# Sigmoid on ScalarE, a last norm in one step, and a ternary layer quantised two tiles ahead

## The reference, cut to what matters

```python
# second layer, attention: a from 12 heads over the tokens, a1 over 100 memory slots
alpha = sigmoid(concat([a, a1]) @ w_alpha + b_alpha)
fused = alpha * a + (1.0 - alpha) * a1
h = h + (fused @ w_proj + b_proj)
# ternary feed-forward, on x = _layernorm(h)
def act_quant(x):
    scale = 127.0 / clip(max(abs(x), axis=-1), 1e-05, None)
    return clip(round(x * scale), -128.0, 127.0) / scale
def bitlinear(x, w, g):              # w is rounded to -1, 0, 1 times one scale
    xn = x * rsqrt(mean(x * x) + 1e-6) * g
    return act_quant(xn) @ weight_quant(w).T
hid = gelu(bitlinear(x, w1, g1))     # 192 -> 768
h = h + bitlinear(hid, w2, g2)       # 768 -> 192
```

## Time and profile before

| what | us |
|---|---|
| median of 3 runs | 1982.28 (1982.16 to 1995.48) |
| the profiled execution | 1991.73 |
| its span, first to last instruction | 1989.9 |
| mean granted clock of TensorE | 0.878 |
| stretch behind attention, pair 1 | 847 to 1028 |
| stretch behind attention, pair 2 | 1810 to 1987 |

### The profile page before, as it was taken

The page is one execution under the profiler, slowest core; times in us unless marked ns, Lnnn a source line. Parts: engine busy times, 40 slices in busy tenths (PEclk is TensorE's granted clock), DMA queues, the critical chain, the costliest instruction groups (busy, mean ns, idle before and its releaser), DMA issues.

```text
span 1989.9 us, 26444 instructions
## 1 busy us (share of the span) xinstructions
PE 1642.2 (83%) x9798; PEld 919.7 (46%) x9798; DVE 1356.8 (68%) x3076; ACT 971.2 (49%) x1383; POOL 126.8 (6%) x165
## 2 busy tenths in 40 slices
PE   0769878998999999964457898799999999999454
PEld 0348646654333333363243584656534333336323
DVE  4668663046889989677768477422588998984876
ACT  0422452124777777732532324330567777775153
POOL 5010000000000000005020100000000000000200
PEclk9977796998999999986568787899989999999656
DMA  6003210016010010001010312000510100100001
GB/s 149 1 1 112 68 44 0 1 35 187 25 32 25 25 32 25 1 1 32 0 33 0 99 45 67 13 0 1 179 60 25 32 25 27 30 9 1 0 0 32
DMA packets 53894, 73.39 MB, mean 37 GB/s; under 512 B 18712, under 2 KB 27205, under 8 KB 53767
## 3 DMA queue, kind: packets, MB, share of 16 engines
q1 hardware_dynamic: 52150, 68.54, 11.9%
q0 software_dynamic: 1616, 3.16, 0.7%
HBM read 38.51 MB, written 33.17 MB: 36 GB/s over the span
## 4 chain that ended last, share of the span: by engine, by line
PE 64%; DVE 26%; ACT 4%; issue 3%; DMA 2%; SPq 1%; POOL 0%; DVEq 0%; ACTq 0%
PE PV L905 9%; PE ST L889 8%; PE S L855 6%; PE ST L801 4%; PE ST L556 4%; PE MT L855 3%; PE PV L914 2%; DVE nmp L1529 2%; DVE Er L1605 2%; DVE st L1402 2%; PE S L812 2%; DVE R L1625 2%; DVE amax L1626 2%; PE ST L586 1%; PE S L850 1%
## 5 line engine op out<-in xcount | busy, mean ns | idle before, releaser
L1232 ACT ACTIVATE Er<-ST 128x1024 f32<-128x1024 f32 x384 | 377.1, 1021 | 106.2 <-PE ST L889 105.9
L1581 DVE TENSOR_REDUCE nmp<-S 128x1 f32<-128x512 f32 x514 | 337.7, 683 | 30.5 <-PE S L855 30.5
L889 PE MATMUL ST<-QS,KS 100*128 100x512 bf16 x768 | 218.0, 385 | 0.3
L905 PE MATMUL PV<-Er,V 128*17 128x512 f32 x1536 | 212.1, 602 | 0.0
L855 PE MATMUL S<-KS,QS 96*128 96x512 bf16 x514 | 183.3, 392 | 0.8
L1581 DVE TENSOR_REDUCE nmp<-MT 128x1 f32<-128x512 f32 x254 | 173.6, 683 | 13.5 <-PE MT L855 13.5
L855 PEld LDWEIGHTS S<-KS,QS 96*128 96x128 bf16 x514 | 48.2, 98 | 154.9 <-DVE nmp L1581 107.2
L450 POOL TENSOR_SCALAR tp<-mv 128x8 f32<-128x8 f32 x20 | 5.2, 258 | 1693.1 <-DVE mv L1406 1693.1
L1529 DVE TENSOR_REDUCE nmp<-S 128x1 f32<-128x512 f32 x120 | 77.5, 684 | 48.3 <-PE S L671 48.1
L889 PEld LDWEIGHTS ST<-QS,KS 100*128 100x128 bf16 x768 | 72.1, 99 | 64.2 <-ACT Er L1232 5.7
L855 PE MATMUL MT<-KS,QS 96*128 96x512 bf16 x254 | 99.4, 391 | 0.9 <-DVE nmp L1581 0.9
(11 more groups left out here) (386 smaller groups left out, 3210.9 us busy)
## 6 DMA issues: line engine op xcount, KB each, us to landing
KS<-scr_k SPq DMA_DIRECT2D x72, 192.0 KB, 2.7
scr_k<-R SPq DMA_DIRECT2D x16, 576.0 KB, 4.0
QS<-scr_q SPq DMA_DIRECT2D x48, 192.0 KB, 2.8
scr_k<-R SPq DMA_DIRECT2D x16, 384.0 KB, 4.6
QS<-scr_k SPq DMA_DIRECT2D x24, 192.0 KB, 2.4
scr_q<-R SPq DMA_DIRECT2D x8, 576.0 KB, 4.5
scr_k<-R SPq DMA_DIRECT2D x16, 192.0 KB, 5.2
scr_q<-R SPq DMA_DIRECT2D x8, 384.0 KB, 4.7
```

What stands on the lines that cost most here:

```text
L889: ins = nc.tensor.matmul(ST[i % 2][:, (kt % 2) * HALF:(kt % 2 + 1) * HALF], KS[0:KP + 4, k, kt * P:(kt + 1) * P], QS[0:KP + 4, k, half * H ...
L905: ins = nc.tensor.matmul(PV[row:row + VC, :], slots[h // H].V[:, kt, h % H, :], E[:, step % RING, (kt % 2) * HALF:(kt % 2 + 1) * HALF], st ...
L1232: A_(E[:, g, :], ST[i % 2][:, :], ACT.Exp).then_inc(s["exps"], 1)
L1581: v.tensor_reduce(nmp[:, u // 2, u % 2:u % 2 + 1], bank, AX.X, ALU.max).then_inc(s["reduced"], 1)
```

## The change

- ScalarE takes Sigmoid instead of exp(-x); VectorE's add of 1 and its reciprocal go. The difference of `U` and `X` is a function of its own (`differ`), made for both slots as soon as a slot's turns (jobs 4 and 5) are done.
- The last norm: `centre` subtracts the mean and multiplies by the weight in one step for each tile (scalar_tensor_tensor) and takes the largest magnitude; it waits for the statistics alone. `quantise` multiplies the magnitude and the scale by `rnn` in small steps, and scales a tile with `MAGIC` added, unlinked; it signals after each half (`scaled`). ScalarE takes `MAGIC` away (`unscale`: Identity with a bias column) for half a slot at a time.
- The order: VectorE adds slot z's projection before slot a's norm. ScalarE makes unscale(a), qcopy(a), unscale(z), Gelu of a's first tile, qcopy(z), Gelu of z's first tile. TensorE makes a's first `bit_up` before z's turns. In the ternary layer VectorE quantises tiles 0 and 1 ahead of the spread of tile 4, and so on.

```diff
--- before.py
+++ after.py
@@ -160,6 +160,7 @@
...
         wsum = sb("wsum", [P, 2])
+        unmagic = sb("unmagic", [P, 1])
@@ -251,7 +252,7 @@
...
             units0 reduced0 units reduced rowmax mturned mcopied acc0 ctxr accout st0 ex0 pv0 ctxn ctxt ctxtc att atts
-            pooled mixin mixed merged stile exps pv alpha alphae fusedx fproj h3 quant qturned qcopied
+            pooled mixin mixed merged stile exps pv alpha alphae fusedx fproj h3 scaled quant qturned qcopied
             vlink plink filled pp pa pd kr0 kr1 kr2 kr3 qr0 qr1 qr2 qr3 q0w q0r mw mr""".split()
@@ -986,7 +987,7 @@
...
                     half, c = i // 2, i % 2
-                    pe.wait_ge(s["quant"], at(p, o, 8, 4 * half + 4))
+                    pe.wait_ge(s["quant"], at(p, o, 2, half + 1))
                     if i >= 2:
@@ -1084,7 +1085,8 @@
...
                     turn_quant(p, o)
-                for t in range(HT):
+                    bit_up(p, o, 0)
+                for t in range(1, HT):
                     for o in slots:
@@ -1249,6 +1251,18 @@
...
+            def unscale(p, o):
+                for half in range(2):
+                    act.wait_ge(s["scaled"], at(p, o, 2, half + 1))
+                    A_(o.XQ[:, HT * half:HT * half + HT, :], o.X[:, HT * half:HT * half + HT, :], ACT.Identity, scale=1.0, bias=unmagic[:, 0:1]).then_inc(s["quant"], 1)
+            def qcopy(p, o):
+                for i in range(4):
+                    half, c = i // 2, i % 2
+                    act.wait_ge(s["qturned"], at(p, o, 4, i + 1))
+                    A_(o.XQT[:, c, half * HALF:(half + 1) * HALF], o.D2[i % 2][0:CH, :].bitcast(BF16)[:, 0:HALF], ACT.Copy).then_inc(s["qcopied"], 1)
             def bit_gelu(p, o, t):
@@ -1318,15 +1332,16 @@
...
                             act.wait_ge(s["fusedx"], at(p, o, 4, i - 1))
-                        A_(o.e2[:, i % 2, :, :], o.D2[i % 2][:, 0:2 * D].rearrange("p (t d) -> p t d", t=2), ACT.Exp, scale=-1.0).then_inc(s["alphae"], 1)
+                        A_(o.e2[:, i % 2, :, :], o.D2[i % 2][:, 0:2 * D].rearrange("p (t d) -> p t d", t=2), ACT.Sigmoid).then_inc(s["alphae"], 1)
                 for o in slots:
                     evac(p, o, 6, o.XT)
-                for o in slots:
-                    for i in range(4):
-                        half, c = i // 2, i % 2
-                        act.wait_ge(s["qturned"], at(p, o, 4, i + 1))
-                        A_(o.XQT[:, c, half * HALF:(half + 1) * HALF], o.D2[i % 2][0:CH, :].bitcast(BF16)[:, 0:HALF], ACT.Copy).then_inc(s["qcopied"], 1)
-                for t in range(HT):
+                unscale(p, a)
+                qcopy(p, a)
+                unscale(p, z)
+                bit_gelu(p, a, 0)
+                qcopy(p, z)
+                bit_gelu(p, z, 0)
+                for t in range(1, HT):
                     for o in slots:
@@ -1351,6 +1366,7 @@
...
+            v.memset(unmagic[:], -MAGIC)
             v.memset(nmp[:], 0.0).then_inc(s["reduced"], 2)
@@ -1595,30 +1611,41 @@
...
+            def differ(p, o):
+                ve.wait_ge(o.s["turned"], p * 28 + 24)
+                for i in range(4):
+                    own, mem = o.U[:, 2 * i:2 * i + 2, :], o.X[:, 2 * i:2 * i + 2, :]
+                    ins = v.tensor_tensor(own, own, mem, ALU.subtract)
+                link(ins)
             def fuse(p, o):
...
                     own, mem = o.U[:, 2 * i:2 * i + 2, :], o.X[:, 2 * i:2 * i + 2, :]
-                    v.tensor_scalar(e, e, 1.0, None, ALU.add)
-                    link(v.tensor_tensor(own, own, mem, ALU.subtract))
-                    link(v.reciprocal(e, e))
                     link(v.tensor_tensor(own, own, e, ALU.mult))
...
+            def centre(p, o):
+                ve.wait_ge(o.s["stats"], p * 5 + 5)
+                for t in range(T):
+                    ins = v.scalar_tensor_tensor(out=o.X[:, t, :], in0=o.HS[:, t, :], scalar=o.mv[:, t, 0:1], in1=g1bc[:], op0=ALU.subtract, op1=ALU.mult)
+                link(ins)
+                link(v.tensor_reduce(o.amax[:], o.X[:], AX.X, ALU.max, apply_absolute_value=True))
             def quantise(p, o):
                 ve.wait_ge(o.s["rstd"], p * 5 + 5)
-                for t in range(T):
-                    ins = v.tensor_scalar(o.X[:, t, :], o.HS[:, t, :], o.mv[:, t, 0:1], o.rnn[:, t:t + 1], ALU.subtract, ALU.mult)
-                link(ins)
-                link(v.tensor_tensor(o.X[:], o.X[:], g1bc[:].unsqueeze(1).to_broadcast([P, T, D]), ALU.mult))
-                link(v.tensor_reduce(o.amax[:], o.X[:], AX.X, ALU.max, apply_absolute_value=True))
+                link(v.tensor_tensor(o.amax[:], o.amax[:], o.rnn[:], ALU.mult))
                 link(v.tensor_scalar(o.qinv[:], o.amax[:], 1e-5, 1.0 / 127.0, ALU.max, ALU.mult))
...
                 link(v.reciprocal(o.qsc[:], o.qinv[:]))
+                link(v.tensor_tensor(o.qsc[:], o.qsc[:], o.rnn[:], ALU.mult))
                 for t in range(T):
-                    link(v.tensor_scalar(o.X[:, t, :], o.X[:, t, :], o.qsc[:, t:t + 1], MAGIC, ALU.mult, ALU.add))
-                    v.tensor_scalar(o.XQ[:, t, :], o.X[:, t, :], MAGIC, None, ALU.subtract).then_inc(s["quant"], 1)
+                    ins = v.tensor_scalar(o.X[:, t, :], o.X[:, t, :], o.qsc[:, t:t + 1], MAGIC, ALU.mult, ALU.add)
+                    if t % HT == HT - 1:
+                        ins.then_inc(s["scaled"], 1)
@@ -1705,36 +1732,48 @@
...
                 for o in slots:
+                    differ(p, o)
+                for o in slots:
                     fuse(p, o)
-                for o in slots:
+                def h3(o):
                     for i in range(4):
...
                     ve.wait_ge(s["h3"], at(p, o, 4, 4))
-                    stats(p, o, o.HS)
-                for o in slots:
-                    quantise(p, o)
+                def both(job, *n):
+                    for o in slots:
+                        job(p, o, *n)
+                h3(a)
+                stats(p, a, a.HS)
+                h3(z)
+                centre(p, a)
+                quantise(p, a)
+                stats(p, z, z.HS)
+                centre(p, z)
+                quantise(p, z)
                 for t in range(HT):
-                    for o in slots:
-                        spread(p, o, t)
-                for o in slots:
-                    scales(p, o, 0)
-                for t in range(HT):
-                    for o in slots:
-                        quantise_hidden(p, o, t)
-                    for o in slots:
-                        spread(p, o, t + HT)
-                    if t % 2 == 1:
-                        for o in slots:
-                            store(p, o, t // 2)
-                for o in slots:
-                    scales(p, o, 1)
-                for t in range(HT, T):
-                    for o in slots:
-                        quantise_hidden(p, o, t)
-                    if t % 2 == 1:
-                        for o in slots:
-                            store(p, o, t // 2)
+                    both(spread, t)
+                both(scales, 0)
+                both(quantise_hidden, 0)
+                both(quantise_hidden, 1)
+                both(spread, 4)
+                both(quantise_hidden, 2)
+                both(spread, 5)
+                both(store, 0)
+                both(quantise_hidden, 3)
+                both(spread, 6)
+                both(spread, 7)
+                both(store, 1)
+                both(scales, 1)
+                both(quantise_hidden, 4)
+                both(quantise_hidden, 5)
+                both(quantise_hidden, 6)
+                both(store, 2)
+                both(quantise_hidden, 7)
+                both(store, 3)
```

## The result

The changed kernel takes 1910.84 us (median of 4 runs, 1903.7 to 1912.41). Beside the kernel before on the same chip (1988.76 us, 4 runs) the ratio is 0.9604, 95% interval 0.9578 to 0.963. Its profiled execution took 1911.3 us with a span of 1909.6.

What follows compares the result with a forecast made beforehand. Behind attention, 177 us per pair form a chain mostly set by VectorE, with ring waits. Savings 16.8 + 3.8 + 15.6 = 36.2 us (second pair) and 35.2 (first), together 71.4 off 1982.3, give 1911; range 1898 to 1930.

Steps and rivals of the forecast that it cites:

- rival (2): Whole execution: runs sit on levels 13 us apart, so the median is 1924 or 1898; chance 0.14.
- How the new order is laid out: Behind attention: engines take lists in order with step distances from the trace; old order's end reached within 1 us.
- Part 1: Fusion: add and reciprocal dropped, difference made earlier, TensorE late next; 16.8 us saved in the second pair.
- Part 2: Last norm: of VectorE's 6.8 us only 3.8 arrive, the rest going into ScalarE's new steps and queue order.
- rival 4: Last norm: VectorE's two-input steps slow GpSimd's inverse deviation, one us per us beyond 4.5; kernel slower, chance 0.01.
- Part 3: Ternary layer's tiles: quantising two tiles ahead removes most VectorE waits; 15.6 us saved in the second pair.
- TensorE's term: Tiles: TensorE at its lower clock, 5.8 us a tile; keeping full clock would gain 2 to 4 a pair.
- The first pair: First pair of sequences: gathers overlap VectorE's quantising, so 1 us less is saved, 35.2 us.
- (3): Tiles: the ring closes elsewhere, tiles keep 10.4 us, total 1942 (1927 with half lost); chance 0.13.
- (5): Last norm gives nothing, since ScalarE's queue takes all that VectorE saves; total 1918.5, chance 0.02.

Runs made afterwards that it cites:

- experiment 6: The changed kernel with the difference back in each quarter of the fusion loop instead of ahead of it; 1919.53 us.
- Experiment 9: The changed kernel with slot a's first tiles ahead of slot z's whole numbers, turns and spreads in the queues; 1900.69 us, 0.9537 of the kernel before.
- run 3: The changed kernel with the old tile order, new fusion and new last norm kept; 1950.32 us, 0.981 of the kernel before.
- run 1: The kernel before with the fusion change alone (Sigmoid, the difference made at the turns); 1954.21 us, 0.981 of the kernel before.

## Why the prediction was right

**The total.** 1911 was forecast and 1910.84 measured, but two errors cancel in that, so the agreement to 0.2 us is luck. The saving was forecast at 71.4 us and was 77.3 in the edited stretches. And I took it off a median of three runs, 1982.3, with two of the lower sort in it; a fourth run moved that median to 1988.76, and nine more runs of the kernel before on one chip had their median at 1991.1. Run again, the changed kernel had 1919.72, 71.4 us under that. By the medians on one chip the saving is 71 to 78 us; the levels of rival (2) moved both kernels, the changed one between 1903.7 and 1929.06 in eight runs.

**How the new order is laid out.** It carried: projection start 35.7 us behind the first turn (forecast 36), z's scaling done 31.6 us behind the projection's start (31), spread z0 36.2 us behind a's last add (35.1), seven spreads of 1.98 behind it, sum of the stretch 139.0 (140).

**Part 1**, forecast 16.8: measured 15.9 up to the projection's start and 0.9 in it, 16.8. TensorE is late next, as said, and its turns and first projection run at the higher clock. The Sigmoid's table load is hidden, with 0.67 us to spare. That VectorE's early differences cost nothing was right, and experiment 6 adds that moving them gains nothing either.

**Part 2**, forecast 3.8: measured 2.7 in pair 2. The terms were right (centre steps 2.72 for 2.7, scale steps 1.93 for 1.9, Identity 0.93 for 0.90); the end of z's scaling is 26.1 us behind a's last add, where I had 25.4. Of these 0.7 us 0.3 are GpSimd's chain (a wait of 1.02 for 0.7, its small steps at 0.46 and 0.43 beside VectorE's two-input steps, the mild form of rival 4); the other 0.4 are spread over VectorE's own list. The last 0.4 of the missing 1.1 us lie in the queues of ScalarE and TensorE between z's scaling and spread z0 (10.05 us for 9.7). That these queues hold VectorE up was my reason for 3.8 instead of 6.8. Experiment 9 bears this out: with slot a ahead another 6.5 us come, though not all of them need be the norm's.

**Part 3**, forecast 15.6: measured 18.0. The mechanism was right (VectorE is late next; its waits 1.85, 0.74 and 1.52 us against my 1.8, 0.2, 1.4 and 2.9), the size of TensorE's term was not: I kept it at the lower clock (2.6 us for eight up products, 5.8 a tile), and it is at the upper one for about half of the stretch (mean 0.75), so that the last waits come to 2.3 us instead of 4.3. The shorter products account for this by their rows; no run holds the clock down with this order. The prediction had this as an end of the range, 2 to 4 us a pair, and not as the value taken.

**The first pair** was not cheaper by 1 us for the gathers, as I had it, but gained 39.9 and in the second execution 36.7 us. Of the 3.1 us between these two, 1.0 lies ahead of the projection, where the second execution starts its turns at the lower clock (1.09 us for four instead of 0.64). The other 2.07 are a wait of VectorE ahead of a spread, behind ScalarE's idle time of 2.60 us ahead of a Gelu whose product was long done. What ScalarE waited for there the trace doesn't say, and it stays open. It is no accident of one execution, though: seven of the eight executions with this queue order have such an idle time of 2.0 to 2.9 us in pair 1, all while GpSimd issues the gathers, and the first execution of the changed kernel is the one without. So part 2 is worth 2.3 us in pair 1 (52.2 in run 3 for 54.5 in run 1), and the 4.4 of the first execution are the exception.

**Rivals.** (3) fell: the ring doesn't close elsewhere, VectorE has nothing but those three waits. (4) has the right price and a condition that isn't met. (5) fell by 2.7 us a pair. (2) is real, as an uncertainty of 10 us and more around any forecast here: the changed kernel's two medians are 9 us apart, its eight runs 25.

## What to carry to other kernels

When an engine's waits form a ring through others, let it work one or two tiles ahead: the ring opens, and here TensorE's granted clock rose with it (0.61 to 0.75), so more was gained than was laid out at the lower clock. When a step is taken off the critical engine, look at the queues of those that consume it: here only 2.7 of 6.8 us came through, and putting the ready slot first in the consumers' lists gave 6.5 more. Before trusting a difference of less than 10 us, cut both executions at the same landmarks and see whether it lies in the stretches that were edited.

## What the runs showed of the hardware that I had not expected

GpSimd's memset of 3.51 us held a VectorE step of 128x4 for 2.69 us instead of 0.17, but not the two-input step ahead of it. A link behind each 128x192 step cost 0.13 us a step (2.81 for 1.93 for eight). The granted clock in the same 50 us of the same kernel was 0.86 in one execution and 0.66 in another (300 to 350 us), and 14.4 of the 17.8 us between the two profiled executions of the changed kernel lie in the two stretches that hold such places.
